# A decoder's attention stack: head normalisation, rotation products, squares and rotation tables rearranged

## The reference

```python
def attn_layer(x, Wqkv, qs, ksc, Wo):
    q, k, v = jnp.split(x @ Wqkv, 3, -1)
    q = l2norm(q) * qs
    k = l2norm(k) * ksc
    q = q * cos * scale + rotate_half(q) * sin * scale
    k = k * cos / scale + rotate_half(k) * sin / scale
    return local_attention(q, k, v) @ Wo
def ffn_layer(x, g, bln, W1, b1, W2, b2):
    a, gate = jnp.split((layernorm(x) * g + bln) @ W1 + b1, 2, -1)
    return a * gelu(gate) @ W2 + b2
for i in range(6):
    x = attn_layer(shift_tokens(x), ...) + x
    x = ffn_layer(shift_tokens(x), ...) + x
```

## Time and profile before

| | |
|---|---|
| median of 3 executions | 1338.29 us (1337.63 to 1340.41) |
| the profiled execution | 1334.07 us |
| its span in the profile | 1332.3 us |
| granted clock of TensorE, mean | 0.954 of full speed |
| PE, DVE, ACT, POOL busy, share of the span | 86%, 71%, 63%, 50% |

### The profile page before, as it was taken

The page is one execution under the profiler, slowest core; times in us unless marked ns, Lnnn a source line. Parts: engine busy times, 40 slices in busy tenths (PEclk is TensorE's granted clock), DMA queues, the critical chain, the costliest instruction groups (busy, mean ns, idle before and its releaser), DMA issues. The chain is left out here.

```text
span 1332.3 us, 25833 instructions
## 1 busy us (share of the span) xinstructions
PE 1143.7 (86%) x9541; PEld 716.3 (54%) x9636; DVE 951.0 (71%) x1207; ACT 834.3 (63%) x1260; POOL 671.2 (50%) x522
## 2 busy tenths in 40 slices
PE   7787879998656898998988998899989989899975
PEld 2222347776224665656555655656555655566541
DVE  2798957776646787877877787867877786877733
ACT  4553446665354667776776767676767667676834
POOL 1555524443326665755655465755555555645510
PEclk9888969999878999999999999999999999999987
DMA  3000035100203443445334442444333532434310
GB/s 108 1 0 0 1 49 198 48 24 1 95 1 79 128 111 77 108 103 132 80 92 105 116 111 72 110 115 121 78 92 102 134 96 69 108 91 110 87 46 16
DMA packets 75507, 107.08 MB, mean 80 GB/s; under 512 B 25347, under 2 KB 31938, under 8 KB 75002
## 3 DMA queue, kind: packets, MB, share of 16 engines
q1 hardware_dynamic: 75386, 105.47, 30.3%
HBM read 30.89 MB, written 0.59 MB: 24 GB/s over the span
## 5 line engine op out<-in xcount | busy, mean ns | idle before, releaser
L1673 POOL TENSOR_TENSOR st_sq_sum<-h 128x512 f32<-128x512 f32 x96 | 130.1, 1355 | 201.4 <-ACT h L1426 201.4
L1677 POOL TENSOR_TENSOR mo_w<-mo_w,x 128x512 f32<-128x512 f32 x96 | 122.3, 1274 | 154.0 <-DVE mo_w L1546 154.0
L1426 ACT ACTIVATE h<-banks 128x1024 f32<-128x1024 f32 x96 | 98.3, 1024 | 144.1 <-PE banks L1270 143.8
L1610 DVE TENSOR_REDUCE st_mx<-banks 128x8 f32<-128x512 f32 x96 | 66.4, 692 | 165.6 <-PE banks L1307 165.2
L1278 PE MATMUL banks<-st_sq_sum,head_ones 128*128 128x512 f32 x192 | 106.6, 637 | 47.9 <-POOL st_sq_sum L1673 46.6
L1556 DVE SCALAR_TENSOR_TENSOR st_turned<-st_rn,mo_w 128x1024 f32<-128x1024 f32 x96 | 124.3, 1295 | 5.9 <-POOL mo_w L1678 5.5
L1545 DVE TENSOR_TENSOR x<-banks,st_scaled 128x1024 f32<-128x1024 f32 x96 | 117.0, 1218 | 15.4 <-ACT h L1426 14.0
L1290 PEld LDWEIGHTS banks<-st_wv,stream 128*128 128x128 f32 x768 | 100.7, 192 | 49.7 <-issue 49.3
L1678 POOL TENSOR_TENSOR mo_w<-mo_w,x 128x512 f32<-128x512 f32 x96 | 122.5, 1276 | 0.0
L1307 PE MATMUL banks<-st_k_blocks,st_qT 128*32 128x128 f32 x3072 | 105.5, 279 | 16.9 <-DMA st_k_blocks<-st_turned 16.9
L1331 PEld LDWEIGHTS banks<-st_p_blocks,st_vs 128*64 128x64 f32 x1536 | 77.8, 137 | 74.2 <-issue 72.9
(11 more groups left out here) (230 smaller groups left out, 2629.2 us busy)
## 6 DMA issues: line engine op xcount, KB each, us to landing
st_qT<-st_turned SPq DMA_DIRECT2D x192, 128.0 KB, 2.4
st_k_blocks<-st_turned SPq DMA_DIRECT2D x384, 64.0 KB, 2.0
st_vs<-st_vn SPq DMA_DIRECT2D x96, 192.0 KB, 2.5
st_w_raw<-in_w_qk SPq DMA_DIRECT2D x12, 512.0 KB, 4.7
st_vs<-st_vn SPq DMA_DIRECT2D x96, 48.0 KB, 2.1
mo_w_all<-gate_rows SPq DMA_DIRECT2D x1, 3072.0 KB, 12.9
st_wv<-in_w_v SPq DMA_DIRECT2D x12, 256.0 KB, 3.0
st_wo<-in_wo SPq DMA_DIRECT2D x12, 256.0 KB, 3.1
```

The costliest lines, as they stand in the source:

```text
L1673: nc.gpsimd.tensor_tensor(sq_sum[:], sq[:, 0, :], sq[:, 1, :], ALU.add).then_inc(sq_summed.sem, 1)
L1677: nc.gpsimd.tensor_tensor(cos_part[:, which, 0, :], cos_part[:, which, 0, :], sin_part[:, 1, :], ALU.subtract).then_inc(add_done.sem, 1)
```

## The change

- **Head normalisation.** `root` writes 1/norm to `NORM_BANK` in PSUM instead of `rn` in SBUF. `normalise_heads` reads it there, and stands first in DVE's step, ahead of the softmax's max. `residual1` follows it, ahead of the max as well. The bank is in use from `head_norm` until `normalise_heads`: PE's `head_norm(h)` waits for `rope_done` of unit h-1 instead of `ln_done`.
- **Squares by halves.** `project` signals after each part, and `square` is two instructions of 128 x 512.
- **Four rotation products** of 128 x 512 instead of two of 128 x 1024, in the order cos part 0, sin part 1, sin part 0, cos part 1. POOL's first sum needs the first two. `project` of part 0 waits for the third product of the unit before, part 1 for the fourth.
- **Two sets of tables.** `scaled` is doubled, and the next layer's four tables are made one at a time at t = 4 to 7, at the end of ACT's step.
- The space for this comes from laying `act`, `xn` and `gate` over tiles of the cross attention (in the profile `cr_bias`, `cr_onehot`, `cr_line`); `onehot` and `line` are declared with 128 partitions for that and used as before.

```diff
         def project(s, h):
-            if product_done.any(s.turn, 2 * h):
-                pe.wait_ge(*product_done.at(s.turn, 2 * h))
             for part in range(2):
                 cols = slice(P * part, P * part + P)
+                if product_done.any(s.turn, 4 * h + part - 1):
+                    pe.wait_ge(*product_done.at(s.turn, 4 * h + part - 1))
...
-            last.then_inc(qk_done.sem, 1)
+                last.then_inc(qk_done.sem, 1)
         def head_norm(s, h):
             pe.wait_ge(*sq_summed.at(s.turn, h + 1))
-            if ln_done.any(s.turn, h):
-                pe.wait_ge(*ln_done.at(s.turn, h))
+            if rope_done.any(s.turn, h):
+                pe.wait_ge(*rope_done.at(s.turn, h))
...
         def square(s, h):
-            ac.wait_ge(*qk_done.at(s.turn, h + 1))
             if sq_summed.any(s.turn, h):
                 ac.wait_ge(*sq_summed.at(s.turn, h))
-            A(sq[:], QK_BANKS, ACT.Square).then_inc(sq_done.sem, 1)
+            for part in range(2):
+                ac.wait_ge(*qk_done.at(s.turn, 2 * h + part + 1))
+                A(sq[:, part, :], ps[:, part, :], ACT.Square).then_inc(sq_done.sem, 1)
         def root(s, h):
             ac.wait_ge(*ln_done.at(s.turn, h + 1))
-            A(rn[:, h % 2, :], rn[:, h % 2, :], ACT.Exp, ...).then_inc(r_done.sem, 1)
+            A(NORM_BANK, rn[:, h % 2, :], ACT.Exp, ...).then_inc(r_done.sem, 1)
-        def scale_table(s, which, ahead):
+        def scale_table(s, which, part, ahead):
             ac.wait_ge(*scale_in.at(s.turn, 16 * ahead + 16))
-            for part in range(2):
-                col = 2 * which + part
-                A(scaled[:, which, :, part, :], ...)
+            if ahead and product_done.any(s.turn, 0):
+                ac.wait_ge(*product_done.at(s.turn, 0))
+            col = 2 * which + part
+            A(scaled[:, (s.turn + ahead) % 2, which, :, part, :], ...)
...
                     copy_out(s, t)
+                if 4 <= t < 8 and not s.last:
+                    scale_table(s, (t - 4) // 2, t % 2, 1)
...
-                if t in (11, 12) and not s.last:
-                    ac.wait_ge(*product_done.at(s.turn, 2 * (t + 4)))
-                    scale_table(s, t - 11, 1)
         def rotate(s, h):
             which = h % 2
-            dv.wait_ge(*sq_done.at(s.turn, h + 1))
+            table = scaled[:, (s.turn + h // 16) % 2, which]
+            dv.wait_ge(*sq_done.at(s.turn, 2 * h + 1))
             dv.wait_ge(*scaled_done.at(s.turn, 4 * (h // 16) + 2 * which + 2))
+            v.tensor_tensor(cos_part[:, which, 0, :], ps[:, 0, :], table[:, 0, 0, :], ALU.mult).then_inc(product_done.sem, 1)
+            dv.wait_ge(*sq_done.at(s.turn, 2 * h + 2))
+            if add_done.any(s.turn, 2 * h - 1):
+                dv.wait_ge(*add_done.at(s.turn, 2 * h - 1))
+            v.tensor_tensor(sin_part[:, 1, :], ps[:, 1, :], table[:, 1, 1, :], ALU.mult).then_inc(product_done.sem, 1)
             if add_done.any(s.turn, 2 * h):
                 dv.wait_ge(*add_done.at(s.turn, 2 * h))
-            v.tensor_tensor(sin_part[:], QK_BANKS, scaled[:, which, 1], ALU.mult).then_inc(product_done.sem, 1)
-            v.tensor_tensor(cos_part[:, which], QK_BANKS, scaled[:, which, 0], ALU.mult).then_inc(product_done.sem, 1)
+            v.tensor_tensor(sin_part[:, 0, :], ps[:, 0, :], table[:, 1, 0, :], ALU.mult).then_inc(product_done.sem, 1)
+            v.tensor_tensor(cos_part[:, which, 1, :], ps[:, 1, :], table[:, 0, 1, :], ALU.mult).then_inc(product_done.sem, 1)
         def normalise_heads(s, h):
-            v.scalar_tensor_tensor(turned[:, h % 4], rn[:, h % 2, :].unsqueeze(1).to_broadcast([P, 2, SEQ]), 1e12, ...)
+            v.scalar_tensor_tensor(turned[:, h % 4], NORM_BANK.unsqueeze(1).to_broadcast([P, 2, SEQ]), 1e12, ...)
...
                 job, stage = s.stage(t)
                 n = t + 1
+                if t >= -3 and s.unit(t + 3):
+                    normalise_heads(s, t + 3)
+                if stage == 0:
+                    residual1(s, job)
                 if t >= -1 and s.unit(n):
                     r = n % 2
...
-                if stage == 0:
-                    residual1(s, job)
-                if t >= -3 and s.unit(t + 3):
-                    normalise_heads(s, t + 3)
...
                 if s.unit(h):
-                    pool.wait_ge(*sq_done.at(s.turn, h + 1))
+                    pool.wait_ge(*sq_done.at(s.turn, 2 * h + 2))
...
-                    pool.wait_ge(*product_done.at(s.turn, 2 * h + 2))
+                    pool.wait_ge(*product_done.at(s.turn, 4 * h + 2))
                     nc.gpsimd.tensor_tensor(cos_part[:, which, 0, :], cos_part[:, which, 0, :], sin_part[:, 1, :], ALU.subtract).then_inc(add_done.sem, 1)
+                    pool.wait_ge(*product_done.at(s.turn, 4 * h + 4))
                     nc.gpsimd.tensor_tensor(cos_part[:, which, 1, :], cos_part[:, which, 1, :], sin_part[:, 0, :], ALU.add).then_inc(add_done.sem, 1)
```

49 lines of the change are left out of this document (25 added, 24 removed).

## The result

The changed kernel takes 1273.59 us in the median (1268.07 to 1277.11, four executions), beside 1337.96 (1336.59 to 1340.41) for the kernel before: a ratio of 0.9513 [0.9475, 0.9551]. The direction was right and most of the places were, the size was not.

A forecast was written before the change was run, and what follows sets the result against it. PE was taken as the bound, working 817.0 of the stack's 924.3 us; its waits were the gain. Terms summed to -50.9, cut 10% to -46: 1334.1 to 1288, plus 4.2 for the median, 1292 us (own range 1280 to 1302).

The forecast's parts named there:

- steps 13 to 15, layers 1 to 5 (weights): Steps splitting the next layer's weights: from 7.94 us to a plain step's 7.1, -12.6 us.
- keys -12: PE's waits for keys go with normalisation first, save 1 us of the longest: -14, less 2, so -12 us.
- the rest of the 46.6: -11: PE's remaining waits for the squares' sum, in plain steps and stage 1, 0.3 to 0.5 each, go: -11 us.
- centred rows -4: PE's 4.4 us of waits for centred rows go, as the normalisation is out of the way: -4 us.
- +2.2: Stage 3: halved squares behind a table load cost ACT 0.2 more, eleven times: +2.2 us.
- +1: Tables made in steps 4 to 7: step 5 gets later by 0.2, five times: +1 us.
- Tables: -10.5: PE's 2.32 us hole behind ACT's two tables shrinks to 0.2, five times 2.1: -10.5 us.
- it is no lever: PE's clock in the stack: at 0.98 of full speed, nothing to gain from it.
- I take off 10% for holes that only move: Whole sum: hand-overs not followed through all sixteen steps, so -50.9 is cut to -46 us.
- Opening: -4: First layer's opening: DVE's cast comes 1.2 us earlier, products in smaller pieces, over seven steps: -4 us.
- Rival B: All of it and more: stages 0 and 3 profit as well (20 us of waits), 1279 us; chance 0.09.
- Rival C: Slower: ring of normalisation, max, subtraction, exp, copies, log, root on DVE and ACT sets the pace, 1358 us; chance 0.05.

The follow-up runs named there:

- whole_squares: Changed kernel with one square of 128 x 1024 again instead of two halves; 1291.95 us, ratio to before 0.968.
- cast_first: Changed kernel with DVE's cast of the weights ahead of the normalisation in the first layer; 1267.45 us, ratio to before 0.950.
- norms_sbuf: Changed kernel with 1/norm written to and read from SBUF again, normalisation still first; 1296.31 us, ratio to before 0.972.
- two_products: Changed kernel with two rotation products of 128 x 1024 again, sine first; 1303.83 us, ratio to before 0.976.
- dsq_first: Changed kernel with ACT's layer norm squares ahead of logarithm and root in stage 0; 1258.95 us, ratio to before 0.943.
- norm_late: Changed kernel with head normalisation and residual behind the softmax's subtraction again, 1/norm still in PSUM; 1300.78 us, ratio to before 0.975.
- tables_alone: Kernel before with only the two sets of tables, made at steps 4 to 7; 1325.42 us, ratio to before 0.991.
- late_sbuf: Changed kernel with normalisation behind the subtraction and 1/norm in SBUF, both taken back together; 1304.54 us, ratio to before 0.978.
- tables_old: Changed kernel with the next layer's tables made at the end of steps 11 and 12 again; 1284.05 us, ratio to before 0.962.
- load_late: Changed kernel with dsq_first's and cast_first's edits, plus ACT's table load moved behind the squares in stages 2 and 3; 1246.90 us, ratio 0.934.

## Where the prediction held and where it failed

What held: the squares' halves give 0.41 a step (whole_squares). The normalisation from PSUM takes 1.225 us, none over 1.3, and the probabilities and the split do not clash with it: 0.73 for the split. The four products take 0.68 each (0.69 forecast); their durations add up to 28 us more than those of the two, but they overlap, so DVE's busy time on them rose by 12 us only. In the plain steps this cost nothing. The tables' hole went to 0.25. The three steps with weights fell to 7.14, 7.15 and 7.04 (7.1 forecast). Stages 0 and 3 gave nothing. PE did not wait for the normalisation through its bank.

What failed is the sizing of the sum. By place, with the measured side from the steps' lengths in all layers:

```
                                            forecast   measured
opening of the first layer                     -4.0       -0.1
step 12, layers 1 to 5 (tables)               -10.5      -17.1
steps 13 to 15, layers 1 to 5 (weights)       -12.6      -13.4
all other steps and the last layer's end      -23.8      -32.8
taken off for holes that only move             +4.9
sum                                           -46.0      -63.4
```

1. **All other steps: "keys -12", "the rest of the 46.6: -11", "centred rows -4", "+2.2" for stage 3 and "+1" for the tables' new place.** The largest error, 9 us. The waits for keys went from 16.9 to 1.7, 15.2 less (the prediction's own reading, all but 1 us of the longest, gives 15.9 and not its 14). Steps 4 to 7 gave 17.9 us, of which 9.2 are keys, so 0.36 a step is left where the profile showed a hole of 0.28. Step 9 gave 1.12, where its two holes were 0.79. One reason that rows show: idle time undercounts a hole, since a matmul behind a stall shows some 0.1 us more of its own (1.13 for the norm matmul, 1.02 without a stall in the kernel after). The plain step's floor was 6.94, not the 7.05 to 7.1 that I took. The centred rows gave 1.5 and not 4, since one wait of 2.9 in the last layer stays. Stage 3 cost 0.65 and not 2.2: the two halves back to back take 1.08 us, not 2 x 0.61.
2. **Tables: -10.5, with "it is no lever" for the clock.** The hole gave 10.3. Behind four of the five holes PE ran at half its clock for 3.4 us, another 5.4 us, and this term was put at nothing. It lay in the trace of before.
3. **"I take off 10% for holes that only move".** 5 us in the wrong direction. Holes did move (copied probabilities +1.9, the layer norm's squares +2.9), but the gains were larger elsewhere. The order and the PSUM input give 33.4 together, where the parts alone give 9.1 and 0.3: here each part removes what makes the other lose.
4. **Opening: -4.** It gave 0 against the kernel before, or 1.7 at the same clock. Its later steps fell by 0.3 to 1.1, but step 0 of the first layer rose by 1.43 and the way to the first scores by 1.1. The cast waits behind the normalisation, and this now for the root: with the cast first, the opening's idle time falls from 10.5 to 7.3 us (cast_first). The clock has the rest.

One price beside the sum was wrong too. Had the contention stayed, the prediction would have added 4.5, for the steps with weights. Norms_sbuf shows 24.3, because the first place puts the normalisation beside the probabilities in nearly every step, which was not looked at.

Rival B had the size nearly (1279), by the wrong places: it paid stages 0 and 3. Rival C looked for a ring through the normaliser and drew the wrong one. The one that bound in two_products and norms_sbuf runs over DVE and POOL alone.

Not settled: why step 9 takes back 0.44 us in dsq_first, why the single key landings in steps 6 and 14 differ between layers and runs, why layer 3's hole before left the clock alone, and what moves the start of the stack by up to 6 us. The lower clock ahead of the stack is part of this (66 us of it in norm_late, which starts at 390.8, and 78 in tables_alone, at 397.3), but not one for one.

## What to carry to other kernels

When several edits feed one ring of hand-overs, price them together and take one back at a time in the finished kernel: each alone showed 0 to 11 us, each taken back 15 to 33. Write out the rings engine by engine with the orders that each variant has: the one that bound here had no instruction of ACT in it. An instruction that is moved to the head of a queue must find its inputs ready and no clash beside it, so check what runs on the neighbour in its new place. Look at the clock by place and not as a mean: a hole of 2.3 us in PE was mostly followed by a stretch at half the clock, and cost half as much again. Once a step has no hole left, look for an engine's order where two results are ready and the one that PE waits for stands last; that was 1.3 us per stage here.

## What the runs showed of the hardware

- A DVE instruction with both inputs in SBUF (1.22 us alone) took up to 2.05 beside a POOL instruction of 1.04 that had started first and was not stretched (norms_sbuf, 82 cases). Where DVE's started first, POOL's was stretched: the squares' sum from 1.27 to as much as 2.05 (late_sbuf, 62 cases), the split of the weights from 0.73 to a mean of 1.48. With one input in PSUM both effects were gone: 1225 ns in all 96 cases, and 0.73 for the split. I had expected the split to suffer, not the normalisation to this extent.
- The granted clock fell to 0.50 for 3.4 us behind four of five idle stretches of 2.32 us on PE (before), two of five (tables_old), and none of five of 0.25 (after). A matmul of 128x512 took 0.63 us there and 0.40 at full clock.
- Instructions back to back overlap: two squares of 0.60 take 1.08 together when both are ready, and DVE's four products of 0.68 start 0.60 apart. A sum of durations overcounts by 0.08 to 0.1 for each. (In the whole run the four products' durations add up to 261 us and keep DVE busy for 238.)
- The root's exp took 692 ns into PSUM where it took 0.72 us into SBUF.
- The squares ran right behind the gelu without the load that the exp needs (load_late).
